# A state-space layer with a mixture of experts: one scan over two channel chunks, three decay banks, three product banks, small sums moved off VectorE

## The reference

```python
x = x + mamba(layernorm(x))
x = x + moe(layernorm(x))

def mamba(x):
    x_ssm, z = split(x @ in_proj_w.T)
    xc = silu(causal_conv(x_ssm, 4 taps) + conv_b)
    B, C, d = split(xc @ x_proj_w.T)          # 16, 16 and 1 columns
    delta = softplus(d)                       # one number per token
    # for each channel and each of the 16 states n, along the 1024 tokens of a batch:
    #   h = exp(delta * A[n]) * h + delta * B[n] * xc
    #   y += C[n] * h
    y = (y + D_param * xc) * silu(z)
    return y @ out_proj_w.T

def moe(x):                                   # 8 experts, the top two of each token
    ...
```

## Time and profile before

| | us |
|---|---|
| median of 3 runs | 2839.52 (2834.74 to 2843.43) |
| the profiled execution | 2832.45 |
| its span, first to last instruction | 2830.4 |
| PE busy | 2346.3 (83%) |
| DVE busy | 2261.3 (80%) |
| POOL busy | 1810.6 (64%) |
| ACT busy | 1483.6 (52%) |
| mean granted clock of TensorE | 0.913 of full speed |

### The profile page before, as it was taken

The page is one execution under the profiler, slowest core; times in us unless marked ns, Lnnn a source line. Parts: engine busy times, 40 slices in busy tenths (PEclk is TensorE's granted clock), DMA queues, the critical chain, the costliest instruction groups (busy, mean ns, idle before and its releaser), DMA issues.

```text
span 2830.4 us, 34513 instructions
## 1 busy us (share of the span) xinstructions
PE 2346.3 (83%) x9510; PEld 1362.2 (48%) x9510; DVE 2261.3 (80%) x3144; ACT 1483.6 (52%) x2417; POOL 1810.6 (64%) x1418
## 2 busy tenths in 40 slices
PE   5667767698998889798897989798887989798886
PEld 2435344454545555454545545454544545454442
DVE  3888888899888989898888989888888988868400
ACT  3554554456474656556564656546564656534231
POOL 2555665657575776757685776757686676748542
PEclk8778777699998999899998999899998999889998
DMA  3772421223233443435343443435344343436875
GB/s 121 250 261 87 138 78 35 80 85 127 83 109 108 121 141 112 124 108 161 98 138 115 115 142 103 136 102 167 96 128 126 107 150 108 127 112 181 215 228 153
DMA packets 192570, 366.27 MB, mean 129 GB/s; under 512 B 22912, under 2 KB 22912, under 8 KB 192384
## 3 DMA queue, kind: packets, MB, share of 16 engines
q1 hardware_dynamic: 144272, 263.26, 29.0%
q0 software_dynamic: 28672, 67.13, 10.9%
q10 hardware_dynamic: 19440, 33.69, 3.3%
HBM read 212.73 MB, written 151.26 MB: 129 GB/s over the span
## 4 chain that ended last, share of the span: by engine, by line
PE 44%; DVE 21%; issue 15%; POOL 8%; ACT 8%; DMA 2%; DVEq 1%; SPq 0%; POOLq 0%; ACTq 0%
PE work L1179 32%; DVE acc L1021 8%; DVE h L1013 8%; PE hT L1184 8%; POOL u L728 6%; ACT decay L874 3%; DVE xc L1044 3%; PE work L1184 2%; PE work L1239 1%; POOL x_out L828 1%; DVE xc L1070 1%; ACT xn L891 1%; ACT x L952 1%; POOL row_scratch L813 1%; ACT L874 1%
## 5 line engine op out<-in xcount | busy, mean ns | idle before, releaser
L728 POOL TENSOR_TENSOR u<-xc,b_ring 128x1024 f32<-128x1024 f32 x512 | 1228.4, 2408 | 747.0 <-DVE h L1013 609.6
L874 ACT ACTIVATE decay<-dt,neg_a 128x512 f32<-128x512 f32 x1024 | 699.6, 688 | 689.6 <-DVE h L1013 661.4
L1184 PE MATMUL hT<-ident,h 128*128 128x128 f32 x4096 | 663.2, 297 | 386.5 <-DVE acc L1021 280.6
L1184 PEld LDWEIGHTS hT<-ident,h 128*128 128x128 f32 x4096 | 503.2, 151 | 658.7 <-DVE acc L1021 328.6
L1021 DVE SCALAR_TENSOR_TENSOR acc<-hT,ct,acc 128x512 f32<-128x512 f32 x960 | 699.6, 729 | 65.4 <-PE hT L1184 63.2
L1013 DVE TENSOR_TENSOR_SCAN h<-decay,h_last,u 128x512 f32<-128x512 f32 x512 | 652.0, 1275 | 113.5 <-ACT decay L874 76.9
L1179 PE MATMUL work<-w_exp,xeT 128*128 x1528 | 709.1, 608 | 35.0 <-issue 25.8
L1013 DVE TENSOR_TENSOR_SCAN h<-decay,u 128x512 f32<-128x512 f32 x512 | 620.6, 1214 | 98.7 <-ACT decay L874 57.2
L1179 PE MATMUL work<-xnT,w_in 128*128 128x512 f32 x1024 | 492.8, 627 | 0.7 <-issue 0.7
L1179 PEld LDWEIGHTS work<-w_exp,xeT 128*128 128x128 f32 x1528 | 279.7, 193 | 342.7 <-issue 342.6
L1179 PEld LDWEIGHTS work<-xnT,w_in 128*128 128x128 f32 x1024 | 198.5, 204 | 207.1 <-issue 207.1
(11 more groups left out here) (143 smaller groups left out, 1840.7 us busy)
## 6 DMA issues: line engine op xcount, KB each, us to landing
b_ring<-b_scratch SPq DMA_DIRECT2D x256, 256.0 KB
xe<-row_scratch SPq DMA_DIRECT2D x165, 256.0 KB
result_scratch<-ye SPq DMA_DIRECT2D x165, 256.0 KB
row_scratch<-x_out ACTq DMA_DIRECT2D x32, 1024.0 KB, 4.9
x<-in_x SPq DMA_DIRECT2D x66, 256.0 KB, 5.0
x_scratch<-x SPq DMA_DIRECT2D x64, 256.0 KB, 3.2
xn<-in_x SPq DMA_DIRECT2D x62, 256.0 KB, 3.0
x_out<-x_scratch SPq DMA_DIRECT2D x44, 256.0 KB, 3.9
```

The source lines that it names most:

```text
L728: nc.gpsimd.tensor_tensor(out=u[:, at:at + 2, :], in0=xc[:, half, 2 * k:2 * k + 2, :], in1=b_ring[:, n % ROWS:n % ROWS + 1, :].to_broadcas ...
L874: nc.scalar.activation(decay_bank[g % 2][:], dt[:, half, :], ACT.Exp, scale=neg_a[:, c, n:n + 1]).then_inc(decay_ready, 1)
L1184: last = nc.tensor.transpose(ps[:, k * P:(k + 1) * P], tile(k), ident[:])
```

## The change

**Scan.** One `tensor_tensor_scan` covers two chunks, 1024 elements: 512 scans in place of 1024, each with `initial` 0. That the second chunk doesn't start from the first one's state is done by data: the decay in column 0 of each bank is zero, set once at the start by DVE, and ACT's `exp` writes the columns 1 to 511 only. In the second block of a batch the state that is carried over comes in through `u`: ACT makes the first decays of all states once (`carry`), POOL multiplies them by `h_last` (in two instructions per such block) and, behind each `u` product, adds two columns to column 0 of `u` (a new instruction of 128x2, 32 per such block), for which it waits for its own product (`u_made`).

**Decay banks.** Three in place of two. A pair of chunks needs two neighbouring banks; pairs take (0,1) and (1,2) in turn. The first decay of a pair goes into the outer bank and may start once the scan before the last one is done; the second goes into bank 1 and waits for the last scan.

**Product banks.** `WORK` is 3, and all tables of places are new.

**Small sums.** `bn_aggr` is gone from DVE (128 instructions). POOL joins the two halves of `bn_stats` itself, with nine small instructions for two quarters in place of four. The router's bias is added on PE by a fifth, one-row matmul, and DVE takes the top values from PSUM. `b_scale` runs on POOL, from `xp_rows`, a new tile that `xp_evict` fills; the product bank of the raw rows is free from then on. `b_store` stands at place 57.52 in place of 51.12, and the load of B for the next block at place 60 as before.

In each pair of pieces below, the first is the kernel before, the second the changed one, in block 7 (a second half), places 16 to 21.

The diff, cut to its core (of the tables two lines are shown):

```diff
-    WORK = 4
+    WORK = 3
...
-        "b_scale": [43.89],
-        "b_store": [51.12],
+        "b_scale": [50.4],
+        "b_store": [57.52],
...
-                steps += [("u", n, c // 2)] * (c % 2 == 0) + [("decay", n, c), ("scan", n, c)]
+                steps += [("u", n, c // 2)] * (c % 2 == 0) + [("decay", n, c)] + [("scan", n, c // 2)] * (c % 2)
...
-        decay_bank = [bank(f"decay{i}") for i in range(2)]
+        decays = ctx.enter_context(nc.psum_tensor("decays", [P, 3, 512], fp32))
...
+        def pair_of(j, n, k):
+            pair = (j * N + n) * C // 2 + k
+            return pair, slice(pair % 2, pair % 2 + 2)
+
+        def decay_of(j, n, c):
+            pair, _ = pair_of(j, n, c // 2)
+            first, bank_no = (((0, 0), (1, 1)), ((1, 2), (0, 1)))[pair % 2][c % 2]
+            return 2 * (c // 2) + first, bank_no, pair - 1 + c % 2
...
-                        nc.gpsimd.tensor_scalar(veps[:, two, :], mv[:, two, 1:2], LN_EPS, None, ALU.add).then_inc(veps_ready, 1)
...
+                        nc.gpsimd.tensor_tensor(out=stat_sum[:, two, :], in0=stat[:, two, 1:3], in1=stat[:, two, 4:6], op=ALU.add).then_inc(stat_step, 1)
+                        nc.gpsimd.tensor_tensor(out=gap[:, two], in0=stat[:, two, 1], in1=stat[:, two, 4], op=ALU.subtract).then_inc(stat_step, 1)
...
-                        wait(pool, scanned, j * N * C + 2 * (g - 1))
+                        if half == 1 and k == 0 and n in (0, N - 1):
+                            part = slice(0, N - 1) if n == 0 else slice(N - 1, N)
+                            pool.wait_ge(first_decays, pair + 1)
+                            pool.wait_ge(h_kept, pair * N + (N - 1 if n == 0 else N))
+                            nc.gpsimd.tensor_tensor(out=carry[:, :, part], in0=carry[:, :, part], in1=h_last[:, :, part],
+                                                    op=ALU.mult).then_inc(carried, 1)
+                        wait(pool, scanned, j * N * C // 2 + g - 1)
...
+                        if half == 1:
+                            if k == 0 and n in (0, N - 1):
+                                pool.wait_ge(carried, 2 * pair + 1 + n // (N - 1))
+                            pool.wait_ge(u_made, pair * N * C // 2 + g + 1)
+                            nc.gpsimd.tensor_tensor(out=u[:, at:at + 2, 0], in0=u[:, at:at + 2, 0], in1=carry[:, 2 * k:2 * k + 2, n],
+                                                    op=ALU.add).then_inc(u_ready, 1)
+                    elif s[0] == "b_scale":
+                        wait_used(pool, j, ("xp_project", 0))
+                        wait_used(pool, j, ("dt_project", 0))
+                        nc.gpsimd.tensor_tensor(out=b_rows, in0=xp_rows[0:N, :], in1=dt[0:N, 1 - half, :], op=ALU.mult).then_inc(b_scaled, 1)
...
-                        wait(act, scanned, j * N * C + g - 1)
-                        nc.scalar.activation(decay_bank[g % 2][:], dt[:, half, :], ACT.Exp, scale=neg_a[:, c, n:n + 1]).then_inc(decay_ready, 1)
+                        c, bank_no, before = decay_of(j, n, c)
+                        wait(act, scanned, before)
+                        nc.scalar.activation(decays[:, bank_no, 1:T], dt[:, half, 1:T], ACT.Exp, scale=neg_a[:, c, n:n + 1]).then_inc(decay_ready, 1)
...
-                        nc.vector.tensor_tensor_scan(out=h[:, n % 2, c, :], data0=decay_bank[g % 2][:], data1=u[:, g % UR, :],
-                                                     initial=first, op0=ALU.mult, op1=ALU.add).then_inc(scanned, 1)
+                        nc.vector.tensor_tensor_scan(out=flat(h[:, n % 2, 2 * k:2 * k + 2, :]), data0=flat(decays[:, banks, :]),
+                                                     data1=flat(u[:, at % 2 * 2:at % 2 * 2 + 2, :]), initial=0.0,
+                                                     op0=ALU.mult, op1=ALU.add).then_inc(scanned, 1)
...
-                        nc.vector.bn_aggr(out=mv[:, q, :], in_=stat[:, q, :]).then_inc(stat_ready, 1)
...
-                        nc.vector.tensor_tensor(out=logit[:, q, :], in0=ps[:, 0:E], in1=b_router[:], op=ALU.add).then_inc(free, 1)
-                        wait_used(dve, j, ("router", q))
-                        nc.vector.max(top_logit[:, q, :], logit[:, q, :]).then_inc(gate_step, 1)
+                        nc.vector.max(top_logit[:, q, :], ps[:, 0:E]).then_inc(gate_step, 1)
...
+                        nc.tensor.matmul(ps[:, 0:E], ones[0:1, 0:1].to_broadcast([1, P]), b_router[0:1, :], start=False, stop=True).then_inc(full, 1)
```

329 lines of the change are left out of this document (176 added, 153 removed).

## The result

| | before | after |
|---|---|---|
| median of 4 runs, us | 2838.86 (2834.74 to 2843.43) | 2927.8 (2925.28 to 2935.78) |
| ratio, 95% interval | | 1.0321 [1.0298, 1.0344] |
| span of the profiled execution, us | 2830.4 | 2923.1 |

The changed kernel is 89 us, 3.2%, slower. The forecast was 60 us faster, with a range up to 2860. Both the sign and the range were wrong.

A forecast was written before the change was run, and what follows sets the result against it. It took DVE to bound fifteen blocks, its saved work counting about one to one. 112 us saved less 52 added by POOL, ACT's tie and banks gave 60 off 2839.5: 2779.5 us, range 2700 to 2860.

The forecast's parts named there:

- long scan: DVE's scans: pairs merged into one save 2.6 us in a first-half block, 6.4 in a second.
- small sums: On DVE, dropping bn_aggr, the bias add and b_scale saves 3.1 us a block.
- POOL +22: Longer norm chains on POOL make DVE wait for u, 1.5 us a block; bounds 0 and 18.5.
- tie of the second decay: ACT's second decay waits for the scan just before, 0.43 us spare; costs 1.3 us a block, at most 6.6.
- three product banks: PE takes a just-emptied bank 5 more times a block; costs 0.7 us a block, at most 3.
- new tables: Tables of the sixteenth block and tail left at zero, either way by some 10 us; no term for the fifteen blocks.
- DVE's work passes into the time about one to one: From blocks 6 and 7: 6.2 us more DVE work, 1.0 us more PE work, 7.6 us longer.
- The scan's own cost: On DVE, a scan of 1024 elements should last 2.27 us, with the next start after 2.18 us.
- DVE's busy time: Sign over the whole run: DVE busy near 2140 us, 2261 less 16 blocks' savings.
- rival 3: ACT's second decay comes late, DVE stops, then PE: 7 more late decays a block, 53 us slower, 2893; chance 18%.
- rival 2: POOL sets the pace: 188 us added there, 40% comes through, 2832 us, no change; chance 12%.
- PE's clock: Sign in a first half: PE's granted clock stays at 0.99 and its busy share is 90%.

The follow-up runs named there:

- e18: Kernel before with only the long scan and what belongs to it; decays and eighth expert's weights left out of the result: 2859.36 us, 1.0083.
- e1: Kernel before with only the small sums moved (bn_aggr, router's bias, b_scale off DVE); old tables, four product banks, single scans: 2856.65 us, 1.0071.
- e16: e15 without the second decay's wait for the last scan: 2873.82 us, 1.0138 of the kernel before.
- e15: e13 with the old tables and four product banks, second decay's tie kept: 2875.15 us, 1.0147 of the kernel before.
- e14: e13 with the second decay waiting only for the scan before the last one: 2925.95 us, 1.0332 of the kernel before.
- e13: Control: changed kernel, decays written aside, scan reading constants, eighth expert's weights left out; all waits kept: 2931.98 us, 1.0350 of the kernel before.
- e17: e13 with the fourth product bank back and the new tables kept: 2932.29 us, 1.0328 of the kernel before.
- e11: Kernel before with each router product made three times on PE: 2955.71 us, 1.0417.
- e5: Changed kernel with two transposes of an expert tile's rows (rows_T) placed later: 2927.01 us, no change.
- e6: e5 with gate_sum and the first two conv steps on DVE placed later: 2971.98 us, 1.0469 of the kernel before.
- e7: Kernel before with the first y_skip moved from place 5.98 to 4.93: 2854.86 us, 1.0061.
- e8: Changed kernel with the norms' sums and router's bias back on DVE, b_scale still on POOL: 2923.72 us, 1.0307 of the kernel before.

## Why the prediction was wrong

The parts, as forecast and as measured, in us of the whole run (the forecast's are its terms times blocks: 66 = 8 x 2.6 + 7 x 6.4, and 46, 22, 20 and 10 are 15 blocks of 3.1, 1.5, 1.3 and 0.7):

| step | forecast | measured | by |
|---|---|---|---|
| long scan | -66 | +24 | e18 against before, by the ratio |
| small sums | -46, POOL +22 | +20 | e1 against before |
| tie of the second decay | +20 | +1 to +6, not clear of noise | e16 to e15, e14 to e13 |
| three product banks, at given places | +10 | 0 (+6 by the ratios), not clear of noise | e17 to e13 |
| new tables | 0 | +57 (+51 by the ratios) | e15 to e17 |
| sum | -60 | +102 to +107 | |

The measured parts add up to 13 to 18 us more than the +89 of the whole; scan and small sums together cost 39 (e16), not 44, and e13 lies 4 to 8 above the kernel after. Each part is known to some 5 to 8 us only.

**"DVE's work passes into the time about one to one": the step that failed.** It was read from two neighbouring blocks, of which the longer had both more DVE work and a lower granted clock; nothing in the pair of rows told the two apart. The runs say otherwise. e1 takes 29 us of DVE's work away in eleven blocks, and they are 19 us longer; e18 takes 28 away, and they are 31 longer; e11 gives PE 144 us more and loses 119. Together the terms that rest on this step were forecast at 90 us off (66 + 46, less POOL's 22), and e16 has them at 39 us on. The engines hold each other by shared banks and a hand-made order, so that a wait taken from one place turns up at another (e5, e14), and 88% busy was no proof that DVE sets the time. Only in blocks 0 to 2, where no expert tile runs, did the saving show: block 1 is 7.0 us shorter. No run changed DVE's work and nothing else, so the price of a microsecond on DVE alone stays unmeasured.

**The scan's own cost was right.** 2.28 us by the row, 2.27 forecast. DVE's busy time was forecast near 2140 us and came to 2191.5. Part of the difference is what e18 shows, 28 us saved in eleven blocks where the slots said 48; some 13 of the missing 20 are small DVE instructions that became long there (token_shift 8, tiles_to 5; last section).

**The new tables: a term that was not in the sum.** The prediction left the tail's tables "either way by some 10 us" and gave the blocks' tables nothing. They are the largest single cost measured, 57 us, though the scan missed its forecast by more (90). With them come new waits of y_skip, prob_sum and the convolution, 80 us in eleven blocks, against 34 us saved at the residual; the waits of y_skip, prob_sum and the convolution stand in e17 and not in e15. So does a tail of 217.8 us where 190 to 205 was forecast. They could have been seen: the diff puts the first y_skip at 4.66 in place of 5.98, soon behind the y_T of PE that it waits for. But e5 and e6 also warn: of the wait at a place only part, or less than nothing, is its price.

**Three product banks.** I counted banks reused within a pair and priced each by an eviction. Given the places that is nothing clear of noise (e17). By the list of steps the cost is rather that three banks do not admit the old places; e7 priced one such place at 17 us.

**The tie of the second decay, and rival 3.** Its time (2893) was nearest, its mechanism was not the cause. DVE's waits for decays rose from 7.0 to 11.8 us a block, between what the forecast (8 to 9) and rival 3 (15) said, but they stay at 11.8 when the tie is gone (e14). With the old tables they come with the small sums (77 to 101 in e1) and shrink when those go back (122 in e16, 87 in e18); in the changed kernel e8, which puts back all but `b_scale`, still has 124. The row of e16:

```profile
DVE h L1073 <- ACT decays_out L931: 121.7, 88, 3.0
```

**POOL, and rival 2.** POOL's adds were priced by a second half's 18.5 us of work. But first halves, which have no adds, grew more (10.7 against 4.6 us). What was missed on POOL: a queue of u behind b_scale's wait for DVE, 4.0 us a block in e1, and carry ahead of a second half's first u, where the scan stands 1.7 us longer. That carry costs "nothing" was wrong. The bias matmul, taken as nothing in PE's spare time, takes 24.9 us of PE in all; e8, which leaves it out of the changed kernel, gains nothing, and what it costs in e1 was not tried.

**PE's clock, a sign that failed.** A first half was to stay at 0.99 with PE at 90%; block 6 ran at 0.94 with PE at 89%. In the eleven blocks most of the growth is PE's busy time, not its idle time: of the changed kernel's 79.6 us, 63.3 (16.9 of them the bias row), and in e18, which has the kernel before's instructions on PE, all of the 31.2 (PE busy 33 us longer, clock 0.94 in place of 0.96). PE's idle time was 228 us before, 245 after and 226 in e18. So the loss comes together with the same products at a lower clock. Whether the waits cost the time and the clock only follows, or the clock carries a part of it, no run tells apart.

**What stays open.** How e1's 20 us divide; which places make up the 57 us; what part PE's clock has; and whether new tables exist for the long scan with which it gains. With the old ones it doesn't, and no version here that does all the kernel's work beats the kernel before.

## What to carry to other kernels

An engine that is 88% busy beside another at 84% need not be the bound: before counting what it saves, add a little work to each engine, or take some away, and see which of them the time follows. Here that was done for PE only. A diff that changes a hand-made table of places has that table as its largest unknown, and a forecast needs a price for it. A wait named in the profile is no price either: take it away and see whether the next one in the queue takes its time.
